# A GRU recurrence cut into halves of its units: two candidate-and-update banks, and the first half's scan ahead of the second half's turning

## What is computed

```python
def cell(h, x):
    gi = x @ W_ih + b_ih
    gh = h @ W_hh + b_hh
    i_r, i_z, i_n = jnp.split(gi, 3, axis=-1)
    h_r, h_z, h_n = jnp.split(gh, 3, axis=-1)
    r = jax.nn.sigmoid(i_r + h_r)
    z = jax.nn.sigmoid(i_z + h_z)
    n = jnp.tanh(i_n + r * h_n)
    h_new = (1.0 - z) * n + z * h
    return (h_new, h_new)
```

## Time and profile before

| | |
|---|---|
| median of 3 runs | 1963.13 us (1960.36 to 1968.94) |
| span of the profiled execution | 1963.7 us |
| start of the recurrence's first turning | 943.8 us |
| start of its last turning | 1904.4 us |
| PE busy share of the span | 93% |

### The profile page before, as it was taken

The page is one execution under the profiler, slowest core; times in us unless marked ns, Lnnn a source line. Parts: engine busy times, 40 slices in busy tenths (PEclk is TensorE's granted clock), DMA queues, the critical chain, the costliest instruction groups (busy, mean ns, idle before and its releaser), DMA issues. The chain is left out here.

```text
span 1963.7 us, 85507 instructions
## 1 busy us (share of the span) xinstructions
PE 1832.6 (93%) x37682; PEld 1269.7 (65%) x37682; DVE 1147.7 (58%) x3364; ACT 785.3 (40%) x2196; POOL 393.5 (20%) x862
## 2 busy tenths in 40 slices
PE   6999999999999999988999999999999999999983
PEld 2433444453444344444998888888888999888861
DVE  5667676766676667343455555555555555555567
ACT  0554565655555565633222222222222222222224
POOL 0121211121111212110122122221222211222113
PEclk7997999999999999989999999999999999999995
DMA  6654443526152623141100000000000000000002
GB/s 160 219 141 126 121 127 85 152 63 181 47 172 67 180 68 93 34 152 42 77 15 10 13 13 13 13 4 13 13 13 13 7 11 13 13 13 12 5 4 86
DMA packets 65377, 127.65 MB, mean 65 GB/s; under 512 B 15401, under 2 KB 22057, under 8 KB 61412
## 3 DMA queue, kind: packets, MB, share of 16 engines
q1 hardware_dynamic: 61372, 120.30, 21.3%
q0 software_dynamic: 3072, 0.82, 0.2%
q10 hardware_dynamic: 560, 1.05, 0.2%
HBM read 77.56 MB, written 37.85 MB: 59 GB/s over the span
## 5 line engine op out<-in xcount | busy, mean ns | idle before, releaser
L439 DVE TENSOR_REDUCE mx<-MX 128x1 f32<-128x512 f32 x768 | 483.3, 683 | 191.7 <-PE MX L568 191.2
L1003 PE MATMUL gate<-whh,state 128*8 128x128 f32 x16384 | 503.8, 273 | 31.5 <-DVE state L919 13.4
L504 ACT ACTIVATE pr<-ST 128x512 f32<-128x512 f32 x768 | 409.5, 596 | 223.5 <-PE ST L588 223.1
L1003 PEld LDWEIGHTS gate<-whh,state 128*8 128x8 f32 x16384 | 430.4, 91 | 87.6 <-DVE state L919 84.7
L896 DVE STREAM_TRANSPOSE trn<-gate 128x128 f32<-128x128 f32 x256 | 81.3, 318 | 337.7 <-PE gate L1003 337.7
L1003 PE MATMUL pg<-whh,state 128*8 128x128 f32 x8192 | 278.4, 273 | 0.3 <-issue 0.3
L951 ACT ACTIVATE rg<-pre 128x32 f32<-128x32 f32 x256 | 58.8, 230 | 504.0 <-DVE pre L898 504.0
L568 PE MATMUL MX<-K,Q 51*128 51x512 f32 (+1 forms) x768 | 242.4, 445 | 15.0 <-DMA Q<-d_q 10.5
L588 PE MATMUL ST<-Q,K 53*128 53x512 f32 (+1 forms) x768 | 240.6, 485 | 13.3 <-ACT pr L504 9.2
L588 PEld LDWEIGHTS ST<-Q,K 53*128 53x128 f32 (+1 forms) x768 | 98.7, 189 | 215.5 <-ACT pr L504 118.9
L1003 PEld LDWEIGHTS pg<-whh,state 128*8 128x8 f32 x8192 | 230.3, 90 | 1.2 <-issue 0.9
(11 more groups left out here) (190 smaller groups left out, 1943.3 us busy)
## 6 DMA issues: line engine op xcount, KB each, us to landing
d_q<-hi_q SPq DMA_DIRECT2D x32, 256.0 KB, 3.5
d_q<-lo_q SPq DMA_DIRECT2D x32, 256.0 KB, 4.0
d_k<-hi_k SPq DMA_DIRECT2D x32, 256.0 KB, 2.9
d_k<-lo_k SPq DMA_DIRECT2D x32, 256.0 KB, 2.9
K<-d_k SPq DMA_DIRECT2D x64, 128.0 KB
Q<-d_q SPq DMA_DIRECT2D x64, 128.0 KB
K<-d_k SPq DMA_DIRECT2D x16, 512.0 KB
Q<-d_q SPq DMA_DIRECT2D x16, 512.0 KB
```

Source lines behind the costliest of these rows:

```text
L439: dve.reduce_max(mx[:, u, col:col + 1], bank[:, :], AX.X).then_inc(mx_red, 1)
L504: act.activation(pr[:, kc % 2, i], ST[n % 3][:, :], ACT.Exp, scale=SCALE[UNITS[w][0]]).then_inc(exped, 1)
L1003: last = pe.matmul(bank[32 * j:32 * j + B, lo:hi], held[q][:, c, :], whh[:, c, o + lo:o + hi], start=first, stop=done)
```

## The change

The 512 units are cut into two halves (64 of each 128). The columns of `whh` are put in another order on the host, so that one bank holds a half's candidate (64 columns) and update gate (64 columns) together: `psA` for the first half, `psB` (two banks) for the second. R stays whole.

- PE: R's chunks 0 and 1, A's chunks 0 and 1, wait for the second half's scan, R's chunks 2 and 3, A's chunks 2 and 3, then all four chunks of B. The number of products is the same. `begin` does each bank with 4 bias products and 4 share products of 64 columns: 16 instructions in place of 8 of 128 columns.
- DVE: R as before; then for the first half a turning (128 columns, candidate and update gate together), multiply, add and scan; then the same four for the second half. The two turnings of Z into PSUM go away.
- ACT: sigmoid of R, then sigmoid of z and tanh of n for the first half, then both for the second half. The sigmoids of z read SBUF now.
- TG goes from 16 to 32 steps: a `piece` multiplies 256 moving columns, there is one in each step in place of two, and the last ones are done 32 steps before the end. `keep` comes every fourth step, with twice the columns. The first block, done before the recurrence starts, is twice as wide.
- POOL's program is as before.

The core of the diff:

```diff
-        TG, TZ, RZ = 16, 16, 3
+        TG, TZ, RZ = 32, 16, 3
@@ DVE
-                    dve.transpose(trn[:, R, :], psR[:, 0:P]).then_inc(s_tr, 1)
...
-                    dve.transpose(trn[:, N, :], psN[:, 0:P]).then_inc(s_tr, 1)
...
-                    dve.tensor_tensor(tmp[:], tr[N], rg[:], ALU.mult).then_inc(s_chain, 1)
...
-                    dve.transpose(turnedZ[0], psZ[q][:, 0:64]).then_inc(s_trz[0], 1)
-                    dve.transpose(turnedZ[1], psZ[q][:, 64:128]).then_inc(s_trz[1], 1)
+                    dve.transpose(trn[:, 2, :], psR[:, 0:P]).then_inc(s_trr, 1)
+                    dve.wait_ge(s_trr, t + 1)
+                    dve.tensor_tensor(pre[:, 0], tr[2], share(t, R), ALU.add).then_inc(s_prer, 1)
+                    def turn(a):
+                        dve.wait_ge(s_ps[a], t + 1)
+                        dve.transpose(trn[:, a, :], half_bank(a, t)[:, 0:P]).then_inc(s_tr[a], 1)
+                    def candidate(a):
+                        dve.wait_ge(s_tr[a], t + 1)
+                        if a == 0:
+                            dve.wait_ge(s_r, t + 1)
+                        dve.tensor_tensor(tmp[:, half(a)], tr[a][:, 0:H], rg[:, half(a)], ALU.mult).then_inc(s_chain, 1)
+                        dve.wait_ge(s_chain, 2 * t + a + 1)
+                        dve.tensor_tensor(pre[:, 1, half(a)], tmp[:, half(a)], share(t, N)[:, half(a)], ALU.add).then_inc(s_pre[a], 1)
+                    turn(0)
+                    candidate(0)
+                    update(0)
+                    turn(1)
+                    candidate(1)
+                    update(1)
@@ ACT
                     for z in range(2):
-                        a.wait_ge(s_trz[z], t + 1)
-                        a.activation(by[:, half(z), :, 2], turnedZ[z].rearrange("p (c m) -> p c m", c=H)[:, :, 0:B], ACT.Sigmoid).then_inc(s_z[z], 1)
+                        a.wait_ge(s_tr[z], t + 1)
+                        a.activation(by[:, half(z), :, 2], tr[z][:, H:C], ACT.Sigmoid).then_inc(s_z[z], 1)
+                        a.wait_ge(s_pre[z], t + 1)
+                        a.activation(sides[q][:, half(z), :, 0:3:2], pre[:, 1, half(z)].rearrange("p c (b v) -> p c b v", v=1).to_broadcast([P, H, B, 2]),
+                                     ACT.Tanh).then_inc(s_n[z], 1)
-                    if blk + 1 < NG and k % 2 == 1:
+                    if blk + 1 < NG and k % 4 == 3:
@@ PE
+                    products(psR, 0, q, NEAR, first=True)
+                    products(psA, 1, q, NEAR)
                     if t > 0:
                         pe.wait_ge(s_h[1], t)
+                    products(psR, 0, q, FAR, done=True).then_inc(s_psr, 1)
+                    products(psA, 1, q, FAR, done=True).then_inc(s_ps[0], 1)
+                    products(psB[q], 2, q, range(C), done=True).then_inc(s_ps[1], 1)
                     if t + 1 < T:
-                        begin(t + 1)
+                        begin(t + 1, 0)
+                        begin(t + 1, 1)
...
-                        piece(blk + 1, 2 * k)
-                        piece(blk + 1, 2 * k + 1)
+                        piece(blk + 1, k)
```

More of the change, by code:

```diff
@@ L733, in recurrent_and_last_layer @@
         trn = sb("trn", [P, GATES, P])
[L734 removed]
+        tr = [trn[:, i, :].rearrange("p (c m) -> p c m", c=C)[:, :, 0:B] for i in range(3)]
         pre = sb("pre", [P, 2, C, B])
@@ L745, in recurrent_and_last_layer, with half_bank @@
         s_z0 = sem("first_shares_ready")
[L746 to L751, removed]
+        R, N = 0, 1
+        s_psr, s_ps = sem("reset_products"), [sem(f"half_products{a}") for a in range(2)]
+        s_trr, s_tr = sem("reset_turned"), [sem(f"half_turned{a}") for a in range(2)]
+        s_prer, s_pre = sem("reset_summed"), [sem(f"candidate_summed{a}") for a in range(2)]
+        s_n = [sem(f"candidate_ready{a}") for a in range(2)]
         s_z = [sem(f"update_ready{a}") for a in range(2)]
         s_h = [sem(f"state_ready{a}") for a in range(2)]
-        psR, psN, zb = ps
+        psR, psA, zb = ps
+        psB = pg[0:2]
         NINIT = 22
-        tR, tN = 0, 1
-        TG, TZ, RZ = 16, 16, 3
+        HW = P // 2
+        def half_bank(a, t):
+            return psA if a == 0 else psB[t % 2]
+        TG, TZ, RZ = 32, 16, 3
         NG, PER = T // TG, 8
         gru = ctx.enter_context(ExitStack())
-        near = gru.enter_context(nc.psum_tensor("near", [P, 512], fp32))
-        turnedZ = [x[:, P:P + 64] for x in (psR, near)]
         giT = gru.enter_context(nc.sbuf_tensor("giT", [P, 2 * TG, 2, C, B], fp32))
@@ L914, in _, with update @@
+                    def update(a):
                         dve.wait_ge(s_z[a], t + 1)
[L915 to L918, removed]
+                        dve.wait_ge(s_n[a], t + 1)
+                        if a == 0 and t > 1:
+                            dve.wait_ge(s_acc, t - 1)
                         dve.tensor_tensor_scan(state[:, 1 - q, W3 * a:W3 * a + W3], by[:, half(a)].rearrange("p c b v -> p (c b v)"), threes(q, a),
@@ L998, in _, with products @@
                 pe.wait_ge(s_init, NINIT)
-                def products(bank, g, q, c, first, done, lo=0, hi=P):
-                    for j in range(4):
[L1002 to L1013, removed]
+                def products(bank, part, q, chunks, first=False, done=False):
+                    for c in chunks:
+                        for j in range(4):
+                            o = part * D + P * j
+                            last = pe.matmul(bank[32 * j:32 * j + B, 0:P], held[q][:, c, :], whh[:, c, o:o + P], start=first and c == chunks[0], stop=done and c == chunks[-1])
+                    return last
@@ new lines, in begin @@
+                def begin(t, a):
+                    n, v = t // TZ, t % TZ
+                    bank = half_bank(a, t)
+                    if a == 0:
+                        if t == 0:
+                            pe.wait_ge(s_z0, 1)
+                        elif n > 0 and v == 0:
+                            pe.wait_ge(s_zd[n % RZ], 192 * (n // RZ + (0 if n % RZ == 0 else 1)))
+                    if t > a:
+                        pe.wait_ge(s_tr[a], t - a)
+                    for j in range(4):
+                        o = P * j + HW * a
+                        pe.matmul(bank[32 * j:32 * j + B, 0:HW], ones_b[:], bnp[:, o:o + HW], start=True, stop=False)
@@ L1019, in begin @@
[L1019 to L1023, removed]
+                        pe.matmul(bank[32 * j:32 * j + B, HW:P], pick[:, B * (v % 4):B * (v % 4) + B], foldZ[:, n % RZ, v // 4, o:o + HW], start=False, stop=False)
+                begin(0, 0)
+                begin(0, 1)
+                NEAR, FAR = range(H), range(H, C)
```

52 lines of the change are left out of this document (16 added, 36 removed).

## The result

The change makes the kernel slower: 2037.9 us (2034.2 to 2051.6, four runs) beside 1963.9 us (1960.4 to 1968.9, four runs), a ratio of 1.040 with an interval of 1.037 to 1.043. That is 74 us more where the prediction had 34. The side was right, and so was the order of the work in a step; one price that is paid three times a step was wrong.

A forecast was written before the change was run, and what follows sets the result against it. Bound: a 3.72 us cycle through PE's products, Z's turning, sigmoid and first scan. From 1963.7 us: steps -3.6, POOL +32.7, start +3.5, first steps +0.5, ends +0.7 gave 1997.5 us; range 1978 to 2014.

The forecast's parts named there:

- Hand-offs are 0.03 us from DVE to DVE and about 0.035 between DVE and ACT: Gaps between dependent instructions in a step's chain, added into the forecast plain step of 3.72 us.
- the halves' prices: Each half's multiply and add 0.175 us in place of 0.19, tanh 0.23; bounds together worth -46 to +31 us.
- the start: First block's pieces twice as wide before the recurrence: 2 to 7 us later, 3.5 taken.
- PE's waits for instructions: PE waiting for its own instructions, 8 us over 239 steps; might hide under the longer chain, half counted.
- 30.7 for POOL: R's add waits for POOL's instruction to end, 0.62, 0.74 or 0.07 us late by part: 30.7 us in all.
- the first 16 steps: Bound by PE with twice the `piece_z`: 0.5 us longer, plus about 2 us from POOL's parts.
- from R's last turning to the last scan: End of the recurrence: 2.98 us in place of 2.47; with R's first turning two groups later, 0.7 us.
- Halves, turnings, cover: A turned under R's sigmoid, B after the first scan; PE covered by 0.15 to 0.27 us a step.
- POOL not on the path (1): Rival: R's add does not wait for POOL on the path; 1965 us, no change; chance 0.10.
- Halves by their columns (2): Rival: halved instructions cost in proportion to columns, PE bounds the step at 3.5 us; 1923 us; chance 0.05.
- DVE emptying between instructions (3): Rival: nothing starts on DVE before the instruction ahead has ended; 38 us more, 2036 us; chance 0.04.
- PE's instruction waits doubling (4): Rival: PE's instruction waits fall uncovered into R's last groups and double; 12 us more, 2010 us; chance 0.06.

The follow-up runs named there:

- Both experiments on the order of the waits: Changed kernel with DVE's last-coming signals waited for first: 2005.4 us; kernel before with the first scan's wait for z written behind the candidate's: 1977.0 us.
- short parts: Changed kernel with POOL's six parts cut to 8 of 512 columns: 2011.4 us.
- waits, turning and bank: Changed kernel with DVE's waits reordered, second half turned ahead of the first half's scan, and R turned into its own PSUM bank: 1969.9 us.
- one opening: Waits reordered, second turning earlier, R's own bank, plus one opening product of 128 columns a quarter bank in place of two of 64 (120 pairs): 1912.1 us.
- the added products of one column: The 120-pair version of the whole computation with eight products of a single column added to each step, 128 pairs again: 1964.7 us.

## Why the prediction was right or wrong

**The step that failed** is "Hand-offs are 0.03 us from DVE to DVE and about 0.035 between DVE and ACT". It was read off instructions whose last signal is their first-written wait and applied to three whose last signal is written second. They take 0.103, 0.088 and 0.101: together 0.187 us more than priced, where the plain step is 0.19 us longer than forecast, 45.4 us over the 239 steps. Both experiments on the order of the waits show the cause. The diff held the information: `candidate` names the sigmoid of R, and `update` names the candidate, behind a signal that comes earlier. The stated range could not catch it: it was made of the halves' prices and the start, and gave the hand-offs no bounds.

**The rest of the sum, over the 239 steps:** 45.4 for the hand-offs, 29.1 for POOL (965.36 against 936.31 with short parts), and 5.5 less for PE's waits for instructions (8.3 us above 239 plain steps before, 2.8 after): 69.0, measured 68.9. These terms are taken from the same runs and have to close; what tests the first is the 0.187 us of the gaps. The prediction had half of the last and 30.7 for POOL. In the first 16 steps it had 2.5, measured 2.6, which is luck: it put about 2 of that on POOL, and with short parts these steps still take 66.45 us, 0.35 less. What else makes them longer no run shows. At the start it had 3.5, measured 3.1; from R's last turning to the last scan 0.5, measured 0.7.

**Halves, turnings, cover.** Their prices held to 0.01 us. A is hidden behind the sigmoid and B comes 0.21 us after the first scan. PE waits for the second scan in mid-step, as forecast.

**Rivals.** POOL not on the path (1): refuted by the long adds and the run with short parts. Halves by their columns (2): refuted, 16 columns cost 0.175. DVE emptying between instructions (3): the predicted time, 2036, is the measured one, but its mechanism is not there: B's turning starts 0.09 us before the scan's end, so a time that fits proves no cause. The Trainium skill, "VectorE: DVE Perf Modes", section "The DRAIN you can't avoid", which the prediction set beside these rows, says that the next operation does not start until the pipeline is empty, and adds in the same paragraph that one which is not held starts earlier. The prediction took over the first half alone; B's turning fits the second. PE's instruction waits doubling (4): the opposite, they hid, and they came back in each faster version.

**What I overlooked about the bound:** I read PE's waits for instructions as 8 us of noise that a longer chain would hide. They are the edge of a second bound that lies right beside the first, and none of the rearrangements on DVE beat the kernel before while the number of pairs stayed at 128.

## What to carry to other kernels

Where a DVE instruction waits for several signals, write the one that comes last first, and price a hand-off by an instruction with the same waits. An operation with two operands in SBUF on the critical path must not fall under a long POOL instruction; one operand in PSUM takes it out. Before rearranging a loop of small matmuls, divide its time by its matmuls: at 30 ns a pair the way to be faster is fewer instructions (wider moving data, one product for two sources), and a better order on the other engines gains only down to that pace.

## What the hardware showed that I had not expected

A second wait on a DVE instruction costs 0.055 to 0.07 us when it is the last to come true, 0.034 us when it comes true 0.04 us ahead of the first, and nothing when it comes true well before.

PE was fed one pair of weight load and matmul each 30 ns on average, although single stretches ran faster: 128 pairs in 3.45 us now and then, 3.76 in the mean with waits, turning and bank. The instruction queue on the page, after and with one opening (packets, MB, share of 16 engines):

```profile
q8 instruction: 297, 4.87, 1.0%
```

```profile
q8 instruction: 281, 4.60, 1.0%
```

A packet is 16.4 KB, and 16 packets fewer go with 2,048 pairs fewer: one for each 128 pairs. The Trainium skill, "Runtime: NRT & Kernel Launch", section "Instruction fetch mechanics", gives blocks of 16 KiB or 256 instructions, with which this agrees, and says that the fetch hides behind the pace at which the sequencer issues. On the last point the traces disagree with it for this loop. The waits that the profile calls issue lie 128 or 129 weight loads apart, or a multiple of that, also where a step has 120 pairs. One with waits, turning and bank:

```profile
1035.05 0.87 PEld L1013 LDWEIGHTS gate<-whh,state 128*8 128x8 f32 x34 [0.50 <-issue]
```

The instruction packet before it runs from 1032.35 to 1033.47 in the trace, so the wait ends 1.57 us behind the packet's end. In steps 16 to 207 all 142 such waits of this version, all 46 of the kernel before and all 33 with one opening end 1.2 to 1.6 us behind the end of a packet of 16,384 bytes, while only 11% of all weight loads start in that range. So PE waits there for a block of instructions to arrive, and not for the pace of issue. With waits, turning and bank the next packet starts 1.24 us behind such a wait, a packet takes 1.06, and a wait ends 1.40 behind its packet (medians). That makes an estimate of 3.70 us for one round of 128 pairs, near the 3.76 of the mean step. That the number of instructions sets the pace, and not their columns, the added products of one column show.
